# Layer 1's matmuls regrouped by operand, hT_lo ahead of agg on VectorE, b3's seed behind layer 1's SiLUs

## What is computed

```python
agg = segment_sum(edge_attr, dst)               # (200000, 48) summed into (12500, 48); dst is sorted
n   = relu(layernorm(x))                        # (12500, 128)
h1  = silu(concat([n, agg], 1) @ W1 + b1)       # 176 -> 256
h2  = silu(h1 @ W2 + b2)                        # 256 -> 256
out = x + n + (h2 @ W3 + b3)                    # 256 -> 128
```

## Time and profile before

| | |
|---|---|
| median of 3 runs | 309.05 us (309.0 to 309.38) |
| profiled execution: its own time | 308.38 us |
| profiled execution: span of the core | 306.5 us |
| TensorE busy | 287.6 us, 94% |
| VectorE busy | 245.6 us, 80% |
| ScalarE busy | 224.8 us, 73% |
| GpSimd busy | 121.6 us, 40% |
| mean granted TensorE clock | 0.983 of full speed |

### The profile page before, as it was taken

The page is one execution under the profiler, slowest core; times in us unless marked ns, Lnnn a source line. Parts: engine busy times, 40 slices in busy tenths (PEclk is TensorE's granted clock), DMA queues, the critical chain, the costliest instruction groups (busy, mean ns, idle before and its releaser), DMA issues.

```text
span 306.5 us, 12286 instructions
## 1 busy us (share of the span) xinstructions
PE 287.6 (94%) x4378; PEld 256.4 (84%) x4379; DVE 245.6 (80%) x620; ACT 224.8 (73%) x435; POOL 121.6 (40%) x240
## 2 busy tenths in 40 slices
PE   6973969999999999999999999999999999999994
PEld 5763849998899889988899888988899888999993
DVE  7788877798887988888888978888888988875560
ACT  8773667778767877778677877779777887779762
POOL 3055534343544345332443435333553435434200
PEclk9996979999999999999999999999999999999999
DMA  5998347556866578555864577555885568731111
GB/s 162 311 289 227 85 129 208 148 155 188 245 180 164 147 233 240 162 140 177 240 194 142 162 220 240 147 151 182 239 228 157 155 192 238 211 95 35 32 31 57
DMA packets 79218, 53.15 MB, mean 173 GB/s; under 512 B 2928, under 2 KB 78794, under 8 KB 79184
## 3 DMA queue, kind: packets, MB, share of 16 engines
q1 hardware_dynamic: 79184, 52.70, 59.8%
HBM read 46.29 MB, written 6.40 MB: 172 GB/s over the span
## 4 chain that ended last, share of the span: by engine, by line
PE 46%; issue 21%; POOL 16%; DVE 8%; POOLq 5%; ACT 1%; DVEq 1%; ACTq 0%
POOL agg_carry L450 12%; PE z L1089 10%; PE agg_ps L1020 10%; POOL rstd L425 4%; PE z L1073 4%; PE z L1077 4%; PE z L1074 4%; POOLq L430 3%; PE z L1053 3%; PE z L1058 2%; PE z L1055 2%; PE z L1059 2%; PE z L1054 2%; PE stage L1024 2%; PE tp L1037 2%
## 5 line engine op out<-in xcount | busy, mean ns | idle before, releaser
L450 POOL TENSOR_TENSOR agg_carry<-staged,agg_carry 48x42 f32 x195 | 80.3, 412 | 79.5 <-POOL agg_carry L450 30.1
L1020 PEld LDWEIGHTS agg_ps<-onehot,raw 128*48 128x48 f32 x1568 | 73.2, 125 | 11.4 <-issue 11.3
L708 DVE TENSOR_TENSOR onehot<-window,rel 128x1176 f32<-128x1176 f32 (+1 forms) x57 | 77.2, 1355 | 5.8 <-DVE stats L683 4.1
L1020 PE MATMUL agg_ps<-onehot,raw 128*48 128x42 f32 x1568 | 77.2, 214 | 1.9 <-DVE onehot L708 1.6
L1024 PE MATMUL stage<-onehot,raw 128*48 128x42 f32 x1560 | 76.9, 214 | 0.0
L425 POOL TENSOR_TENSOR rstd<-vareps,minus_half 112x4 f32<-112x4 f32 (+1 forms) x28 | 38.6, 1377 | 89.2 <-DVE vareps L693 89.2
L1024 PEld LDWEIGHTS stage<-onehot,raw 128*48 128x48 f32 x1560 | 72.8, 125 | 0.1
L1089 PE MATMUL z<-w,h 128*112 128x128 f32 (+1 forms) x448 | 56.1, 278 | 0.8 <-ACT h L563 0.8
L1089 PEld LDWEIGHTS z<-w,h 128*112 128x112 f32 (+1 forms) x448 | 50.5, 176 | 2.4 <-ACT z L555 1.1
L534 ACT ACTIVATE xn<-x_t,nmr,rstd 112x128 f32<-112x128 f32 (+1 forms) x112 | 45.8, 479 | 2.2 <-DVE nmr L701 2.2
L542 ACT ACTIVATE hT_hi<-tp 128x448 fp32r<-128x448 f32 (+1 forms) x28 | 15.2, 544 | 42.7 <-PE tp L1037 42.6
(11 more groups left out here) (119 smaller groups left out, 435.8 us busy)
## 6 DMA issues: line engine op xcount, KB each, us to landing
raw<-in_edge_attr_dram SPq DMA_DIRECT2D x55, 672.0 KB, 5.5
x_t<-in_x_dram SPq DMA_DIRECT2D x27, 224.0 KB, 6.2
out_dram<-out_t SPq DMA_DIRECT2D x27, 224.0 KB, 5.8
dst_rows<-in_dst_dram SPq DMA_DIRECT2D x1, 512.0 KB
raw<-in_edge_attr_dram SPq DMA_DIRECT2D x1, 288.0 KB, 3.5
dst_rows<-in_dst_dram SPq DMA_DIRECT2D x1, 256.0 KB, 2.8
out_t<-in_L_gnn_W_dram SPq DMA_DIRECT2D x1, 256.0 KB, 7.4
x_t<-in_x_dram SPq DMA_DIRECT2D x1, 192.0 KB
```

Source lines behind the costliest of these rows:

```text
L450: pool.tensor_tensor(into, staged[:, parity, k // 2, :], into, ALU.add).then_inc(s_odd, 1)
L708: return dve.tensor_tensor(onehot[:, slot, at * PER:n * PER, :], window[:, :].unsqueeze(1).broadcast_to([P, cols_n, WINDOW]), cols.unsquee ...
L1020: mm = pe.matmul(banks[0:ED, bass.ds(offsets[(k - first) // 2], WINDOW)], edges, into, start=False, stop=True, skip_group_check=True, tile ...
```

## The change

It has three edits. In layer1, the three matmuls with x are issued for both halves before any of the four with the sums, and the wait for agg_lo stands between the two sets. On VectorE, relu_lo moves ahead of carry_over, agg_lo directly behind carry_over, and finish behind agg_lo. On ScalarE, activate2 is cut in its halves: half 0, then clear_bank, then half 1, then activate1, and seed_b3 comes only after activate1.

```diff
-            def activate2(t):
+            def activate2(t, m):
                 n = PER * nodes_p(t)
-                for m in range(M):
-                    act.wait_ge(s_z2, M * t + m + 1)
-                    wait(act, s_z3, t)
-                    act.activation(h2[:, m, 0:n], z[:, m, 0:n], ACT.Silu,
-                                   bias=b2c[:, m:m + 1]).then_inc(s_h2, 1)
-                    if m == 0:
-                        seed_b3(t)
+                act.wait_ge(s_z2, M * t + m + 1)
+                wait(act, s_z3, t)
+                act.activation(h2[:, m, 0:n], z[:, m, 0:n], ACT.Silu,
+                               bias=b2c[:, m:m + 1]).then_inc(s_h2, 1)
...
                     relu(i - 1)
                     split_agg(i - 1)
                 if has(i, 2, NT):
-                    activate2(i - 2)
+                    activate2(i - 2, 0)
                 if has(i, 1, NT - 2):
                     act.wait_ge(s_carried, i)
                     clear_bank(1 - parity)
+                if has(i, 2, NT):
+                    activate2(i - 2, 1)
                 if has(i, 1, NT):
                     activate1(i - 1)
+                if has(i, 2, NT):
+                    seed_b3(i - 2)
...
                 if has(i, 1, NT):
+                    relu_lo(i - 1)
                     carry_over(i - 1, 1 - parity)
+                    agg_lo(i - 1)
                 if has(i, 3, NT):
                     finish(i - 3, 1 - parity)
-                if has(i, 1, NT):
-                    relu_lo(i - 1)
-                    agg_lo(i - 1)
...
                     pe.matmul(z[:, m, 0:n], w1x_hi[:, cols], hT_lo[:, 0:n], start=False, stop=False)
-                    if m == 0:
-                        pe.wait_ge(s_agg_lo, t + 1)
+                pe.wait_ge(s_agg_lo, t + 1)
+                for m in range(M):
+                    cols = slice(m * P, (m + 1) * P)
                     pe.matmul(z[:, m, 0:n], w1e_hi[:, cols], agg_hilo[:, 0:n], start=False, stop=False)
                     pe.matmul(z[:, m, 0:n], w1e_lo[:, cols], agg_hilo[:, 0:n],
                               start=False, stop=True).then_inc(s_z1, 1)
```

## The result

The changed kernel takes 341.51 us (median of 4 runs, 340.91 to 342.59) against 309.02 us: a ratio of 1.105, 95% interval 1.102 to 1.108. The forecast was 340 us, with 67% on its case. The profiled execution took 341.62 us, its span is 339.8.

What follows compares the result with a forecast made beforehand. TensorE's work plus its waits, chiefly for hT_lo, bound the kernel. Steps +25.0 and ends +0.7 and +5.7 gave +31.4 on the 306.5 us span, 337.9, with overheads about 340 us; range 328 to 351, 67% on this case.

Steps and rivals of the forecast that it cites:

- Agg's place: On VectorE, agg behind hT_lo starts 1.14 us after relu's start instead of 0.45, 0.69 us later.
- R: The start of relu on ScalarE in a step, from which the prediction counts times in us.
- R to L: Part of a step from relu's start to layer 1's next start: 3.00 us instead of 2.38, +0.62 a step.
- L: The start of layer 1 on TensorE in a step, from which the prediction counts times in us.
- Half 1's wait: In layer 1, TensorE waits 0.32 us for half 1's SiLU plus a restart of 0.1: 0.42 lost a step.
- the first wait: Sign: layer 1's first matmul waits for ScalarE's SiLU, not for hT_lo, over 0.5 us each time.
- The steps: Steady steps on TensorE take 10.85 us against 9.81: +1.04 each, times 24 is +25.0 us.
- the slack of 0 to 0.4: GpSimd's early additions end by L + 8.6 to 9.0, agg is wanted at L + 8.99: hidden by 0 to 0.4.
- Rival 3: GpSimd's additions become last; two slowed ones put agg 0.3 to 0.6 later: +11, 351 us; chance 9%.
- The ends: Outside the steady steps: +0.7 us into the third layer 1 and +5.7 at the end.
- the term of 2.5: From the last but one layer 1 to the last: layer 3 waits for the seed, +1.9, and R to L, +0.6.
- Rival 4: TensorE's clock could drop from 2.4 to 1.2 GHz through idle of 0.6 and 0.4 a step; no chance given.

Runs made afterwards that it cites:

- e5: The changed kernel with layer 2's SiLU of half 0 ahead of split_agg on ScalarE; 328.0 us.
- e11: The kernel before with VectorE's new order alone, but the output addition (finish) in front of hT_lo instead of behind agg_lo; 325.5 us.
- e8: The changed kernel with clear_bank behind both SiLUs of layer 2 instead of between them; 333.0 us.
- e4: The changed kernel without VectorE's new order, which stays as before; 337.1 us.
- e3: The kernel before with ScalarE's new order alone; 313.7 us.
- e1: The kernel before with VectorE's new order alone; 353.1 us.
- e7: The kernel before with the output addition (finish) ahead of carry_over on VectorE; 304.8 us.
- e6: The changed kernel with seed_b3 ahead of layer 1's SiLUs (activate1); 335.1 us.
- e2: The kernel before with TensorE's regrouped layer 1 matmuls alone; 316.8 us.
- e10: The kernel before with the output addition ahead of carry_over, both layer 2 SiLUs ahead of seed and clear, and TensorE's regrouping; 315.6 us.

## Why the prediction was right, step by step

**Agg's place.** Predicted: agg at R + 1.14, R to L 3.00 instead of 2.38. Measured 1.12 and, in the mean, 3.02; single steps lay between 3.00 and 3.11. The gap from hT_lo to agg, taken as 0.55 between 0.5 and 0.64, is 159.46 - 158.91 = 0.55. e5 shows that the queue on ScalarE carries it, and e11 that this alone makes 16 us.

**Half 1's wait.** Predicted 1.04 between the halves and 0.42 lost; measured 0.94 and 7.76 - 7.41 = 0.35 in the mean of all 24 steps, 7.68 - 7.41 = 0.27 without the first and the last two. The term was 0.07 to 0.15 too large. The SiLU of half 1 starts where it was forecast, at L + 0.28, but half 1 follows it by 0.66 (161.62 to 162.28) and not by the 0.76 that was taken over from half 0. e8 takes the wait away. The sign named for the first wait, over 0.5 us each time, was not met: TensorE's waits for it are 11.2 us in 19, one of them 2.7, since its own stop inside layer 2 took a part of the time.

**The steps.** From the third layer 1 to the last but one, 312.71 - 54.09 = 258.62 us, against 234.15 before: +24.5, predicted +25.0. That this agrees so well is in part luck. From the fourth layer 1 to the 25th (289.54 - 64.92 = 224.62 against 267.23 - 61.97 = 205.26) the 21 steps grew by 0.92 each, not by 1.04. The step before these 21 grew by 1.36, and the two behind them by 3.75 together (289.54 to 312.71 against 267.23 to 286.65), where 2.1 was predicted: in the first TensorE stops 0.66 us for issue in front of layer 3 (296.01), and in the second ScalarE normalizes two tiles, and relu (309.71) starts only as the second one ends, at 309.69. Before, the same work was hidden: relu still waited 0.33 us for the transposes there (284.39).

**The hidden parts.** Stage_sums ended at L + 7.14 (predicted 7.25), and GpSimd's last early addition at 169.95, 0.15 ahead of agg at 170.10, inside the slack of 0 to 0.4. Rival 3 stayed just out; e4, which takes hT_lo out of the way, meets it at once. The three additions ran in 0.25 to 0.27 us each there, since no one-hot lay over them (GpSimd's timeline, against the earlier trace rows):

```profile
168.73 0.25 POOL L450 TENSOR_TENSOR agg_carry<-staged,agg_carry 48x42 f32 x1 [1.04 <-ACT staged L503]
169.15 0.27 POOL L450 TENSOR_TENSOR agg_carry<-staged,agg_carry 48x42 f32 x1 [0.17 <-POOL agg_carry L450]
169.68 0.27 POOL L450 TENSOR_TENSOR agg_carry<-staged,agg_carry 48x42 f32 x1 [0.25 <-POOL agg_carry L450]
```

By the rule of the Trainium skill (SBUF — State Buffer, "SBUF: two separate sides") that VectorE with two SBUF inputs locks GpSimd out for a whole instruction, they should run at their short time once the one-hots are over; the rows agree.

**The ends.** Predicted +0.7 into the third layer 1 and +5.7 at the end. The distance from the second to the third layer 1 grew by 1.9 (54.09 - 41.16 = 12.93 against 52.50 - 41.46 = 11.04), while the second came 0.3 earlier. 0.9 of it is one stop of TensorE inside that step's sums, which the profile puts down to issue; its cause stays open. From the last but one layer 1 to the last it grew by 4.1 (324.41 - 312.71 against 294.29 - 286.65), predicted 2.5; behind that, by 3.2 as predicted (339.8 - 324.41 = 15.4 against 12.2). Together -0.3 + 1.9 + 24.5 + 4.1 + 3.2 = 33.4, against 33.3 between the spans. What was mis-sized at the end is the term of 2.5: a layer 3 at half clock is what it lacked. TensorE's timeline, then stretches with busy time of the engines and the granted clock (first value behind POOL's):

```profile
317.53 3.55 PE L1090 MATMUL z<-w,h 128*112 128x128 f32 x16 [1.71 <-ACT z L555]
```

```profile
312.70:317.50 4.80, 3.10 (x34) 2.58 (x34) 2.49 (x4) 3.19 (x7) 1.13 (x3) 1.00 0.17 48
317.50:321.00 3.50, 3.47 (x17) 3.48 (x18) 0.14 (x1) 0.41 (x1) 0.27 (x1) 0.54 0.02 5
```

After TensorE had stood for 1.71 us, layer 3 ran at a granted clock of 0.54, so nearly all at 1.2 GHz, and took 3.55 us where it takes 2.00 at 2.4 GHz. The same stands in e3 at 299.47, 3.67 us behind a stop of 1.80. The 1.5 us is what the term of 2.5 fell short by.

The length of the stop alone does not decide it. In e4, e5 and e8 the same layer 3 follows a stop of 1.70 or 1.71 us and takes 2.00 us; there it is the next one that is slow, 3.76, 3.35 and 3.52 us behind a stop of 2.44. In the changed kernel this next one follows a stop of 2.44 us too (328.95) and takes 2.00. E4's TensorE timeline:

```profile
312.75 2.00 PE L1091 MATMUL z<-w,h 128*112 128x128 f32 x16 [1.71 <-ACT z L555]
...
322.28 3.76 PE L1091 MATMUL z<-w,h 128*112 128x128 f32 x16 [2.44 <-ACT z L555]
```

So each of these profiled executions has one slow layer 3, and which of the two stops brings it is not explained by these runs. Rival 4 came true, but only there; in the steady steps, with waits of at most 0.7 us, the granted clock stayed at 1, and in e1 too, with two stops of about 0.6 and 0.75 us in each step. The Trainium skill (TensorE: Matmul & The Clock Gate, Part 1) has the clock fall when TensorE idles; the slow ones agree, but by these rows idling for 1.7 or 2.4 us may or may not be enough.

**Parts don't add.** Alone the edits cost 44.7, 8.4 and 5.3 us, together 58; the change cost 32.5. 28 of VectorE's 44.7 us come through the seed between the SiLUs (e1 against e11), and the change moves just that seed away. With e11's 16.2 us in its place the three add up to 29.9, near the 32.5.

## What to carry to other kernels

An operand needed late can still gate a step early: follow not who reads it, but what is queued behind the instruction that waits for it, and on which bank that queued instruction holds the next engine. When two layers share PSUM banks in turn, the matmuls of half 0 are the cover for the read of half 1's bank; regrouping them shortens that cover even if it adds no work. Where other work stands between a wait and the result that the critical path wants, move that work in front of the wait (the output addition in e7, 1.3% faster) before changing the order of what is waited for.

## What was not expected

Removing the costliest edit (44.7 us alone) from the change gave back 4.4 us, because a limit through another engine lay 0.2 us a step below. (The two times are from different comparisons; both periods, 10.78 and 10.59, say the same.) And a wait for the seed was followed in five kernels (the change, e3, e4, e5, e8) by one layer 3 at a granted clock near half, which cost another 1.4 to 1.8 us, while other stops of the same length left the clock at 1.

In the changed kernel TensorE's weight loads also stop 10.7 us in 20 waits inside layer 2 for "issue", against 0.2 before:

```profile
PEld z L1074 <- issue: 10.7, 20, 1.0
```

The stop is between layer 2's halves, where the code reads the sums' offsets into registers. In the changed kernel it hides under the wait for the SiLU: the SiLU ends 0.15 us ahead of layer 1 in each steady step. In e5 it is not hidden: the halves' first matmuls are 1.55 us apart (153.75 and 155.30) where they are 1.31 apart in the kernel before, and R to L is 2.54 where steps without the stop have 2.25. The reads alone are not the cause, since every kernel has them. E4, e5 and e8 have the stop as often (21, 20 and 19 times), but e6, which differs from the change only in the seed's place, has it 2 times, e3 once, and e2 and e10 3 times each. So it comes where the late seed and the regrouping stand together; why, stays open.
